# Scatter on stacked half-precision parts, inverse sums moved to two other places, and one copy split over two engines

## The reference

```
u = _ln_t(t)
logits = u @ gate_w.T + gate_b
probs = softmax(logits, axis=1)
topv, topi = top_k(probs over the tokens, 8), for each of the 16 experts
pooled = sum over the 8 tokens of topv * u[topi]
h = gelu(concat(pooled, 1) @ weight1[e])
out = concat(h, 1) @ weight2[e]
outputs[topi] += out * topv
t = t + outputs
```

## Time and profile before

| | |
|---|---|
| median of 3 runs | 368.87 us (368.51 to 368.97) |
| the profiled execution's own time | 368.35 us |
| its span, first to last instruction | 366.5 us |
| PE busy | 327.2 us, 89% |
| DVE busy | 260.1 us, 71% |
| ACT busy | 183.9 us, 50% |
| POOL busy | 128.8 us, 35% |
| chain that ended last | PE 77%, DVE 10%, DMA 5% |
| mean granted clock of TensorE | 0.948 |

### The profile page before, as it was taken

How to read it: one execution, slowest core, us unless ns; L and a number is a source line. 1 busy time by engine, 2 the same in 40 slices (tenths; PEclk the granted TensorE clock), 3 DMA queues, 4 the chain that set the end, 5 groups by cost and what they waited for, 6 DMA issues and landing times.

```text
span 366.5 us, 8381 instructions
## 1 busy us (share of the span) xinstructions
PE 327.2 (89%) x3362; PEld 249.3 (68%) x3362; DVE 260.1 (71%) x523; ACT 183.9 (50%) x251; POOL 128.8 (35%) x96
## 2 busy tenths in 40 slices
PE   2289998799999999999899999999996986979985
PEld 1168886587777878786678787777774544546774
DVE  2679779957757877869686876776988786454632
ACT  1043355446557574757663755576564547440500
POOL 6134535332444337554211557312235400351000
PEclk9999999999999999999999999999999899995655
DMA  4910100001011010101000101011021100100122
GB/s 125 204 36 3 26 19 16 16 16 31 16 18 26 5 32 2 31 4 32 15 16 2 31 15 17 17 16 26 7 58 32 31 2 18 28 2 29 57 75 69
DMA packets 35906, 11.16 MB, mean 30 GB/s; under 512 B 24431, under 2 KB 35741, under 8 KB 35869
## 3 DMA queue, kind: packets, MB, share of 16 engines
q1 hardware_dynamic: 33152, 9.98, 11.3%
q10 hardware_dynamic: 2717, 0.66, 1.2%
HBM read 5.72 MB, written 4.21 MB: 27 GB/s over the span
## 4 chain that ended last, share of the span: by engine, by line
PE 77%; DVE 10%; DMA 5%; issue 3%; ACT 2%; POOL 1%; ACTq 1%; SPq 0%; DVEq 0%; POOLq 0%
PE psB L892 14%; PE psA L892 13%; PE psB L1025 9%; PE psB L1005 8%; PE psA L990 7%; PE psA L1070 4%; PE psA L882 3%; PE psA L1048 3%; PE psB L1039 3%; DVE negmax L757 2%; PE psA L993 2%; PE psA L983 2%; PE psA L1032 2%; PE psB L1008 2%; PE psB L977 2%
## 5 line engine op out<-in xcount | busy, mean ns | idle before, releaser
L757 DVE TENSOR_REDUCE negmax<-psA 128x1 f32<-128x512 f32 (+7 forms) x128 | 90.5, 751 | 32.2 <-PE psA L993 31.6
L587 ACT ACTIVATE Pp<-psB 128x1024 f32<-128x1024 f32 (+1 forms) x80 | 73.6, 937 | 35.3 <-PE psB L1008 30.7
L892 PE MATMUL psB<-xin,UU 128*128 128x224 f16 (+1 forms) x480 | 56.4, 277 | 0.1
L892 PE MATMUL psA<-y,DD 128*128 128x224 f16 (+1 forms) x480 | 55.1, 273 | 0.0
L990 PE MATMUL psA<-zK,yQ 128*128 128x512 f16 (+1 forms) x192 | 47.8, 332 | 6.0 <-DVE uT L775 2.4
L892 PEld LDWEIGHTS psB<-xin,UU 128*128 128x128 f16 x480 | 47.0, 99 | 7.9 <-DVE xin L698 0.5
L1005 PE MATMUL psB<-yQ,zK 128*128 128x512 f16 (+1 forms) x192 | 47.3, 330 | 3.7 <-DMA yQ<-rows 2.4
L892 PEld LDWEIGHTS psA<-y,DD 128*128 128x128 f16 x480 | 46.7, 98 | 5.5
L477 POOL TENSOR_TENSOR zrstd<-zrstd,power 128x8 f32<-128x8 f32 x16 | 27.2, 1698 | 53.9 <-DVE zrstd L735 53.9
L557 ACT ACTIVATE y<-psB 128x1024 f16<-128x1024 f32 x16 | 16.4, 1023 | 44.8 <-PE psB L892 44.8
L499 POOL TENSOR_TENSOR y<-y 128x1024 f16<-128x1024 f32 x16 | 34.1, 2132 | 9.8 <-ACT y L560 9.8
(11 more groups left out here) (158 smaller groups left out, 504.5 us busy)
## 6 DMA issues: line engine op xcount, KB each, us to landing
x_all<-in_x_dram SPq DMA_DIRECT2D x4, 512.0 KB, 3.9
normalised_tokens<-z SPq DMA_DIRECT2D x16, 128.0 KB, 1.8
zV<-normalised_tokens SPq DMA_DIRECT2D x64, 32.0 KB, 2.1
out_dram<-x_all SPq DMA_DIRECT2D x8, 256.0 KB, 2.3
yQ<-rows SPq DMA_DIRECT2D x32, 2.0 KB
Pp<-filter_tables ACTq DMA_DIRECT2D x4, 121.9 KB, 3.7
w_halves<-y SPq DMA_DIRECT2D x12, 32.0 KB, 1.8
cst<-shape_constants SPq DMA_DIRECT2D x1, 326.5 KB, 4.3
```

The source lines that it names most:

```text
L587: nc.scalar.activation(Pp[:, n % 2, UOFF[e[2]]:UOFF[e[2]] + N], slot(e)[:, 0:N], ACT.Exp).then_inc(b_drained, 1)
L757: ins = nc.vector.tensor_reduce(negmax[:, n % 2, m - 1:m], s[:, at:at + P * m], X, ALU.max, negate=True)
L892: ins = nc.tensor.matmul(within(out_cols, -shift), m, within(v, shift), start=i == 0, stop=i == len(matrices) - 1)
```

## The change

**Two copies of the rows.** gateT, lg, probs, rest and what hangs on them have 128 partitions for 64: the 64 rows twice, one below the other. The logits' weights are 128 columns wide for that, and gate_b is loaded eight times for four.

**The scatter in fp16.** A new event, split, stands after wT in each group: ScalarE copies the routed rows to fp16 (w16), sorted so that a tile of tokens lies contiguous, which writes in steps of 128 elements; on the lower 64 partitions VectorE then puts there what the fp16 copy left (row minus copy). obd has 128 partitions (TensorE turns each part twice) and gets a high part and, on 64 partitions, a low part in fp16. A scatter tile is then two fp16 matmuls: both parts of the rows by the high part, and the high part of the rows by the low part of obd, into one accumulation, sorted by image as t is.

**The inverse sums.** ScalarE no longer scales the exponentials (route had done that). wT multiplies by per_sum, an identity times the inverse sums, which VectorE makes in select, and obd is multiplied by them.

**The last copy of uT** is halved: VectorE takes the first 512 columns, ScalarE the others, and the second logits matmul waits for ScalarE's (uT_second).

**The order.** In LAST both halves of scatter 2 stand behind route, and scatter (0, 0) behind wT; ten fillers ahead of the first experts for five.

```diff
-FILL = {("experts", 0): 5, ("turned", 0): 2, ("scatter", 1, 0): 3}
+FILL = {("experts", 0): 10, ("turned", 0): 2, ("scatter", 1, 0): 3}
...
-            for b in range(GB):
+            for b in range(2 * GB):
                 sp.dma_start(gb_sb[E_ * b:E_ * b + E_, :], gate_b.rearrange("(e a) -> e a", a=1)).then_inc(proj_loaded, 16)
...
-                elif name == "route":
-                    act.wait_ge(inverse_ready, n + 1)
-                    nc.scalar.activation(probs[:, :], probs[:, :], ACT.Copy, scale=inverse[:, 0:1]).then_inc(p_scaled, 1)
+                elif name == "split":
+                    act.wait_ge(route_ready, n + 1)
+                    nc.scalar.activation(by_place(w16[:, n, :]), by_token_row(xF_all[:, n, :]), ACT.Copy).then_inc(w_high, 1)
                 elif e == ("uT", G - 1):
...
+                    to, of = uT_views(slot(e))
+                    nc.scalar.activation(to[:, 1], of[:, 1], ACT.Copy).then_inc(uT_second, 1)
...
                     dve.wait_ge(lg_exp, n + 1)
-                    nc.vector.reciprocal(inverse[:, :], esum[:, :]).then_inc(inverse_ready, 1)
+                    if n >= 1:
+                        dve.wait_ge(a_filled, A["wT", n - 1] + 1)
+                    link(nc.vector.reciprocal(inverse[:, n:n + 1], esum[:, :]))
+                    link(nc.vector.tensor_scalar(per_sum[:, :], ident[0:GE, 0:GE], inverse[0:GE, n:n + 1], None, ALU.mult))
+                elif name == "split":
+                    dve.wait_ge(w_high, n + 1)
+                    v = by_place(w16[GE:P, n, :])
+                    nc.vector.tensor_tensor(v, by_token_row(xF_all[GE:P, n, :]), v, ALU.subtract).then_inc(w_split, 1)
...
-                        ins = nc.vector.tensor_tensor(obd[:, g, :, :], s[0:GE, C * g:C * g + C].unsqueeze(1).broadcast_to([GE, GB, C]),
-                                                      blocks(GB, C, GE, C_BDE), ALU.mult)
-                    ins.then_inc(a_drained, 1)
+                        ins = nc.vector.scalar_tensor_tensor(out=obd[:, g, :, :], in0=s[:, C * g:C * g + C].unsqueeze(1).broadcast_to([P, GB, C]),
+                                                             scalar=inverse[:, g:g + 1], in1=blocks(GB, C, P, C_BDE), op0=ALU.mult, op1=ALU.mult)
+                    link(ins)
+                    link(nc.vector.tensor_copy(obd_high[:, groups, :, :], obd[:, groups, :, :]))
+                    nc.vector.tensor_tensor(obd_low[:, groups, :, :], obd[0:GE, groups, :, :], obd_high[0:GE, groups, :, :],
+                                            ALU.subtract).then_inc(a_drained, 1)
...
                 elif name == "wT":
                     pe.wait_ge(route_ready, n + 1)
-                    ins = turn(s, by_tile(xF_all[0:GE, n, :]), ident[0:GE, 0:GE], GE)
+                    tile = by_tile(xF_all[0:GE, n, :])
+                    for k in range(KT):
+                        ins = nc.tensor.matmul(s[:, GE * k:GE * k + GE], tile(k), per_sum[:, :], start=True, stop=True)
...
                     pe.wait_ge(a_drained, A["turned", n // (G - 1)] + 1)
-                    tile = by_tile(xF_all[0:GE, n, :])
+                    pe.wait_ge(w_split, n + 1)
+                    places = s.rearrange("p (b k c) -> p k b c", b=GB, k=R)
                     for k in range(R):
-                        ins = nc.tensor.matmul(s[:, P * k:P * k + P], tile(R * e[2] + k), obd[:, n, :, :], start=True, stop=True)
+                        tile = w16[:, n, P * (R * e[2] + k):P * (R * e[2] + k) + P]
+                        nc.tensor.matmul(places[:, k], tile, obd_high[:, n, :, :], start=True, stop=False)
+                        ins = nc.tensor.matmul(places[:, k], tile[0:GE], obd_low[:, n, :, :], start=False, stop=True)
```

More of the change, by code:

```diff
@@ L47 @@
 UP_SCALE = DOWN_SCALE = 64.0
+OUT_SCALE = 1024.0
 PACK = [[8], [7, 1], [6, 2], [5, 3], [4]]
@@ L135 @@
         batch(0, "prob", 1), group(4, "proj", 1), batch(1, "score", 0), group(6, "select"),
-        group(6, "logit_exp"), batch(5, "up"), once(13, "w1", 0), group(7, "wT"), batch(0, "prob", 2),
+        group(6, "logit_exp"), batch(5, "up"), once(13, "w1", 0), group(7, "wT"), group(7, "split"), batch(0, "prob", 2),
         once(2, "image", 2), once(6, "image", 3), once(1, "gn_var", 2), group(3, "mean", 0), once(18, "mean", 3, 1),
@@ L147 @@
 LAST = [("proj", G - 1, 2), ("hidden", 0), ("mean", G - 1, 2), ("experts", 0), ("dev", G - 1, 2), ("turned", 0), ("scale", G - 1, 2),
-        ("scatter", 1, 0), ("uT", G - 1), ("scatter", 1, 1), ("logit_max", G - 1), ("logits", G - 1), ("select", G - 1), ("scatter", 2, 0),
-        ("logit_exp", G - 1), ("route", G - 1), ("scatter", 2, 1), ("scatter", 0, 0), ("wT", G - 1), ("pool", G - 1), ("scatter", 0, 1),
+        ("scatter", 1, 0), ("uT", G - 1), ("scatter", 1, 1), ("logit_max", G - 1), ("logits", G - 1), ("select", G - 1), ("logit_exp", G - 1),
+        ("route", G - 1), ("scatter", 2, 0), ("scatter", 2, 1), ("wT", G - 1), ("split", G - 1), ("scatter", 0, 0), ("pool", G - 1),
+        ("scatter", 0, 1),
         ("hidden", 1), ("experts", 1), ("turned", 1), ("scatter", G - 1, 0), ("scatter", G - 1, 1)]
-FILL = {("experts", 0): 5, ("turned", 0): 2, ("scatter", 1, 0): 3}
+FILL = {("experts", 0): 10, ("turned", 0): 2, ("scatter", 1, 0): 3}
 FILL_PV = (0, 5, 2, 1, 2)
@@ L263, in hybrid_kernel @@
         u = sb("u", [P, KT, P])
-        lg = sb("lg", [GE, S])
-        probs = sb("probs", [GE, S])
-        rest = sb("rest", [GE, S])
-        top16 = sb("top16", [GE, 2 * TOP])
-        top8 = sb("top8", [GE, TOP])
-        ntop = sb("ntop", [GE, 1])
-        esum = sb("esum", [GE, 1])
-        inverse = sb("inverse", [GE, 1])
+        lg = sb("lg", [P, S])
+        probs = sb("probs", [P, S])
+        rest = sb("rest", [P, S])
+        top16 = sb("top16", [P, 2 * TOP])
+        top8 = sb("top8", [P, TOP])
+        ntop = sb("ntop", [P, 1])
+        esum = sb("esum", [P, 1])
+        inverse = sb("inverse", [P, G])
+        per_sum = sb("per_sum", [GE, GE])
+        w16 = sb("w16", [P, G, S], F16)
         wT = sb("wT", [P, KT, GE])
@@ L290, in hybrid_kernel @@
         o2 = sb("o2", [C, B, E_])
-        obd = sb("obd", [GE, G, GB, C])
+        obd = sb("obd", [P, G, GB, C])
+        obd_high = sb("obd_high", [P, G, GB, C], F16)
+        obd_low = sb("obd_low", [GE, G, GB, C], F16)
         early = Pp[:, :, :].rearrange("p i n -> p (i n)")
@@ L1038, in _ @@
                     for i in range(2):
-                        ins = nc.tensor.matmul(s[0:GE, BANK * i:BANK * i + BANK], gateT[:, :, :], uT[:, BANK * i:BANK * i + BANK], start=True, stop=True)
+                        if i == 1 and n == G - 1:
+                            pe.wait_ge(uT_second, 1)
+                        ins = nc.tensor.matmul(s[:, BANK * i:BANK * i + BANK], gateT[:, :, :, :], uT[:, BANK * i:BANK * i + BANK], start=True, stop=True)
                         if i == 0:
@@ L1064, in _ @@
                     for g in range(PARTS[n][0] // GB, PARTS[n][1] // GB):
[L1065 removed]
+                        for half in (slice(0, GE), slice(GE, P)):
+                            ins = nc.tensor.matmul(s[half, C * g:C * g + C], o2[:, GB * g:GB * g + GB, :], ident[0:C, 0:C], start=True, stop=True)
                 elif name == "scatter":
                     pe.wait_ge(a_drained, A["turned", n // (G - 1)] + 1)
[L1068 removed]
+                    pe.wait_ge(w_split, n + 1)
+                    places = s.rearrange("p (b k c) -> p k b c", b=GB, k=R)
                     for k in range(R):
[L1070 removed]
+                        tile = w16[:, n, P * (R * e[2] + k):P * (R * e[2] + k) + P]
+                        nc.tensor.matmul(places[:, k], tile, obd_high[:, n, :, :], start=True, stop=False)
+                        ins = nc.tensor.matmul(places[:, k], tile[0:GE], obd_low[:, n, :, :], start=False, stop=True)
                 else:
```

51 lines of the change are left out of this document (31 added, 20 removed).

## The result

| | before | after |
|---|---|---|
| time, us, median (range) | 368.69 (367.94 to 368.97) | 395.12 (392.99 to 397.48) |
| ratio, 95% interval | | 1.0723 (1.0695 to 1.0752) |
| the profiled execution's own time and span, us | 368.35, 366.5 | 396.27, 394.5 |

A forecast was written before the change was run, and what follows sets the result against it. Until about 325 us any TensorE wait is paid in full; behind it stands one chain of dependent steps. 368.35 + 4.45 (body) - 4.6 (end) = 368.2 us; range from the bounds 366.0 to 370.8, with rivals 364.0 to 372.0.

The forecast's parts named there:

- Edits at nothing: Doubled partitions, wider logits weights, gate_b loads (bound 0.6 us) and fillers cost no time; ScalarE's removed route pass gives -0.4 us.
- The split in steps 7 and 11: Body: TensorE waits for rows behind ScalarE's copy and VectorE's subtraction, +2.8 us (2.0 to 3.5) and +1.5 (0.75 to 2.0).
- rival 2: Slower: TensorE's wait in step 7 lets the clock fall in the body, price 1.65 us, 371.0 us; chance 0.15.
- Step 15: Body's last split, with VectorE idle before wT and the mean's square delayed: +0.55 us, bounds 0.2 and 1.3.
- (a): End, experts' outputs to logits: first scatter half 0.9 us, uT's copy halved over two engines, logits start 1.7 us earlier.
- (e): End, last scatter: 16 fp16 matmuls at the lower clock take 1.8 us instead of 4.07, -2.3 us.
- (b): End: ScalarE's pass between reciprocal and selecting product goes, per_sum takes its place, -0.95 us.
- (d): End: last turned gets a second matmul, and obd a cast and a subtraction of 128 columns, +0.75 us.
- (c): End: hidden stands behind one more scatter half, which gets 1.3 us shorter; taken as -0.4 us.
- rival 1: With ten fillers the clock stays at its upper level through the logits, saving 3.2 us, 365.0 us; chance 0.25.
- Rival 3: Scatter outputs written as four runs of 32 columns hold TensorE back, 371.4 us; chance 0.05.

The follow-up runs named there:

- the bench: Not the kernel: 1024-column fp32-to-fp16 copies at various steps on ScalarE and VectorE, and eight 64x64 weight tiles on TensorE as transposes and products; no kernel time.
- the run with gate_b's loads moved: Changed kernel with contiguous split writes, wT by transposes, and gate_b's second four loads issued behind x's second group: 377.41 us (1.0242).
- the repaired kernel: Changed kernel with split's order and place, wT's transposes, gate_b's loads and equal heights (zero rows in obd's low part) put right: 364.40 us (0.9881).

## Why the prediction was wrong, step by step

The prediction failed in two terms of its sum: it gave the split's passes 1.15 and 1.98 us, and they take 4.75 and 4.71; and it put wT's new products at nothing, and they take 3.9 us for 1.17 and are followed by the lower clock. Put right alone, the passes gave 4 us and the products none; put right together they gave 16.

The sum was forecast as 4.45 us in the body against 4.6 at the end. Paid were 24.8 and 3.2 (by the spans). In the order of the prediction:

- **Edits at nothing.** Twice the partitions were free, as said (the route product takes 1.23 us on 128 rows, 1.22 on 64). gate_b's loads were not: bounded at 0.6 us, they cost 1.3: with them x's second load is issued at 8.81 us for 6.95, beside the filter tables, which land later (5.1 us from issue for 3.7). And one edit was not costed at all: wT by the diagonal instead of the identity. I read it as the same eight products; a transpose is one record a tile and takes 1.17 us, a product two, and 3.9. Behind it pool and the convolution ran at the lower clock, and behind transposes they did not. In the bench the same products between streams of 512 columns did not lower it (1.00 there, and behind them), so what in the kernel made it fall is not settled. Beside the long passes all this was hidden (the run with transposes alone gave nothing); without them it is worth some 12 us (391.21 against 378.66, of two sessions; by the ratios 11.8).
- **The split in steps 7 and 11.** The path was right: TensorE waits for the drain of rows, put down to it by name, and all behind the split on VectorE is late by it. The step that failed is the one that took uT's 1.98 us for VectorE and 1.15 for ScalarE. uT's row steps through 4-byte elements; w16 is written in 2-byte elements, and the bench has 4.7 us for ScalarE's copy and for the subtraction. The bounds, 1.22 to 1.98 and 1.15 to 1.87, were drawn from rows without a single fp16 write in steps: they were no bounds. With both passes at 2.0 us and wT by transposes step 7 cost 5.3 us and not 2.8 to 3.5, since the clock fell behind the wait (3.18 us of waiting, then 0.55 of the clock for 3.8 us, 1.7 us lost). That is my rival 2 with its place and price (1.65), and its 15 in 100 was too little. Step 11 cost 2.2 there (forecast 1.5, at most 2.0). In the change as it stood, though, the clock fell ahead of the wait, behind wT's products, and behind the wait of 2.64 us it was at 1.00: there rival 2 is not the account.
- **Step 15** had 0.55 us, and the change paid 8.4. None of that is TensorE waiting for the split: it is wT's products and the lower clock. With both put right the step cost 1.2 us (15.18 before, 16.34 in the run with gate_b's loads moved), within the bounds of 0.2 to 1.3. With transposes and the long passes it cost 6.6; TensorE then waited 2.03 us for exponentials behind the long copy on ScalarE, a path that the prediction did not price, and 1.46 us for those behind the mean's square, for which it had taken 0.3.
- **The end, (a) and (e).** Sized by eight fp16 transposes of one height, the scatter half was to take 0.9 us and took 1.75; the last two 3.6 and not 1.8. The repaired kernel shows the term as it was meant: with equal heights the first half takes 0.8 us, the logits start 11.6 us behind the fillers and not 13.2 (forecast: 1.7 earlier), the last two halves take 1.9 us. What the sum left out altogether is the stretch from wT to pool, 3.6 us longer in the change and 0.6 in the repaired kernel.
- **(b)**, the removed pass: in the change's own end the product ends 1.71 us behind the reciprocal's start, before 2.59; 0.9 as forecast. **(d)**: from the last turned product to the first scatter product 1.50 us in the repaired kernel, before 0.70: 0.8, forecast 0.75. **(c)** and the rest: the repaired kernel's end is 37.3 us, 4.6 under the 42.0 of before. This is the forecast to a tenth, but by luck and other parts: its logits run in part at the upper clock (2.31 us for 3.65), which I had left to rival 1.
- **Rival 1** (the clock holds by ten fillers): the point that was to decide it, the clock in the first scatter, says no (0.50 from 357.0 to 358.7 us), and five fillers for ten change nothing. **Rival 3** (runs of 32 columns): no, 377.46 against 377.41. What it foresaw, a slow scatter, came from the heights.

The stated bounds do not add up either. The body's terms give 2.55 to 6.4 (7 only with gate_b's 0.6), the end's -3.4 to -5.5, and 368.35 with the stated outer bounds is 365.7 to 372.6 and not 366.0 to 370.8. None of this comes near 395.

The chances were placed as though every price were known within a factor of two. The range held the rivals that I had thought of, and not the case that a price had no row.

## What to carry to other kernels

An operation whose form (width of element, step, product or transpose, rows) stands in no row of the trace has no bounds from that trace: a bench of a few instructions settles it before it is placed on a path. Two costs that lie side by side hide each other; taking one away alone shows nothing, so both have to be tried together before either is acquitted. Work that is needed only at the end belongs where its engines are idle, not where its input happens to be ready.

## What the hardware did that I had not expected

- fp16 written in steps of 16 to 256 bytes: 4.5 to 4.75 us for 1024 columns on ScalarE (1.06 contiguous), 2.3 to 2.45 as a cast on VectorE (0.69); fp32 in such steps 1.93 to 2.0 and 1.03 to 1.07. Reads of fp32 in such steps cost 1.9 to 2.0 and 1.0 to 1.07 us.
- fp16 products of 128 columns that alternate between 128 and 64 rows stand 0.16 us apart at the upper clock and 0.22 at the lower; of one height, whichever, 0.055 and 0.107. Sixty-four rows of zeros made a scatter half cheaper by half (0.8 us for 1.75).
- In the run with transposes alone TensorE stood still for 8.6 us in step 7, three times as long as in the change, and the step was 2.4 us longer although VectorE was done at the same time: the 4 us behind that standstill ran at 0.50, where in the change the clock was back at 1.00 behind 2.64 us of standing still.
